# Emptying PSUM bank by bank in three projections, and all weight evacuations of one FFN group on one engine

## What is computed

```python
xn = _layernorm(x, axis=-1)
s = _L0_attn_ref(xn, ...)          # 16 heads, causal softmax, rope on q and k
g = _silu(_L0_ffn_ref(xn, w_gate, w_up, w_down))   # int weights / 127, hidden 3072
x = x + s * g
xn = _layernorm(x, axis=-1)
s = _L1_attn_ref(xn, ...)          # q = x@Wq+bq, k, v alike; softmax(exp(-|q-k|^2)) @ v, then Wo
g = _silu(_L1_ffn_ref(xn, W, b, ids, weights))     # out = sum_k weights[k] * (W[ids[k]] @ x) + bias
x = x + s * g
```

## Time and profile before

| | us |
|---|---|
| median of the 2 runs shown | 3195.87 (3165.48 and 3226.27) |
| profiled execution | 3163.04 |
| its span on the slowest core, core 2 | 3161.5 |
| spans of the 8 cores | 3139.5 to 3161.5 |
| mean granted TensorE clock of the 8 cores | 0.781 to 0.787 |
| TensorE matmuls busy | 2298.7 (73%) |
| VectorE busy | 890.7 (28%) |
| ScalarE busy | 846.7 (27%) |

### The profile page before, as it was taken

How to read it: one execution, slowest core, us unless ns; L and a number is a source line. 1 busy time by engine, 2 the same in 40 slices (tenths; PEclk the granted TensorE clock), 3 DMA queues, 4 the chain that set the end, 5 groups by cost and what they waited for, 6 DMA issues and landing times.

```text
span 3161.5 us, 39763 instructions; the slowest of 8 cores (3139.5 to 3161.5 us)
## 1 busy us (share of the span) xinstructions
PE 2298.7 (73%) x15302; PEld 1261.2 (40%) x15302; DVE 890.7 (28%) x1705; ACT 846.7 (27%) x1181; POOL 78.3 (2%) x148
## 2 busy tenths in 40 slices
PE   2699999984676646787776777347678767887877
PEld 0344444432233213464664666125457322333333
DVE  4344444431232264433223111420110002112122
ACT  2111111112111145464443444201110213222222
POOL 0011111000000000000000000000000000000000
PEclk8799999997878855656556555679889988988899
DMA  4222222202111020101001000441216012011010
GB/s 139 27 34 36 34 33 33 31 1 57 17 17 17 1 53 2 61 2 61 2 1 61 2 2 2 151 109 61 72 57 197 1 27 53 1 54 35 19 54 27
DMA packets 58554, 129.70 MB, mean 41 GB/s; under 512 B 7673, under 2 KB 15867, under 8 KB 55812
## 3 DMA queue, kind: packets, MB, share of 16 engines
q1 hardware_dynamic: 34052, 92.56, 8.7%
q0 software_dynamic: 24320, 34.61, 7.4%
HBM read 142.88 MB, written 18.88 MB: 51 GB/s over the span
## 4 chain that ended last, share of the span: by engine, by line
PE 58%; ACT 16%; DVE 13%; issue 7%; DMA 5%; DVEq 0%; ACTq 0%; SPq 0%; POOL 0%; PEldq 0%; POOLq 0%
PE PS L903 8%; PE PS L737 7%; ACT EB L925 6%; PE PS L1209 6%; PE PS L609 5%; PE PS L618 5%; PE PS L1367 5%; PE PS L1181 4%; PE PS L1436 4%; PE PS L652 4%; PE PS L1292 2%; DVE PS L908 2%; ACT PRJ L745 2%; DVE ACC L663 1%; PE PS L969 1%
## 5 line engine op out<-in xcount | busy, mean ns | idle before, releaser
L903 PE MATMUL PS<-Q,K 64*128 64x128 bf16 x2176 | 274.0, 304 | 126.0 <-ACT EB L925 120.9
L925 ACT ACTIVATE EB<-PS,negBh 128x1152 bf16<-128x1152 f32 (+7 forms) x128 | 204.1, 1594 | 258.0 <-DVE PS L908 242.2
L903 PEld LDWEIGHTS PS<-Q,K 64*128 64x128 bf16 x2176 | 211.4, 135 | 154.8 <-issue 144.1
L1209 PE MATMUL PS<-XN,W1FULL 128*128 128x512 bf16 x768 | 182.3, 399 | 60.6 <-ACT Q L1224 18.7
L652 PE MATMUL PS<-HT,WDT 128*128 128x512 bf16 x768 | 196.4, 392 | 34.8 <-DVE HT L635 21.9
L737 PE MATMUL PS<-XN,WBLK 128*128 128x512 bf16 x768 | 210.4, 442 | 10.1 <-DVE Q L752 5.1
L1181 PE MATMUL PS<-identw,PLAND 128*128 128x128 f32 x1024 | 144.3, 310 | 98.8 <-DMA PLAND<-Wsel 67.3
L908 DVE TENSOR_TENSOR PS<-PS,trinegT 128x128 f32<-128x128 f32 x256 | 76.6, 299 | 440.9 <-PE PS L903 435.0
L1181 PEld LDWEIGHTS PS<-identw,PLAND 128*128 128x128 f32 x1024 | 140.3, 224 | 104.8 <-issue 104.5
L609 PE MATMUL PS<-XN,WGT 128*128 128x512 bf16 x768 | 171.1, 381 | 7.3 <-DVE ACC L663 5.6
L618 PE MATMUL PS<-XN,WUT 128*128 128x512 bf16 x768 | 169.7, 379 | 0.0
(11 more groups left out here) (165 smaller groups left out, 2505.0 us busy)
## 6 DMA issues: line engine op xcount, KB each, us to landing
PLAND<-Wsel SPq DMA_DIRECT2D x64, 512.0 KB, 4.4
XF<-xT SPq DMA_DIRECT2D x8, 1024.0 KB, 12.9
XT<-xT SPq DMA_DIRECT2D x4, 2048.0 KB, 8.7
x1park<-XT SPq DMA_DIRECT2D x32, 256.0 KB
X1CH<-x1park SPq DMA_DIRECT2D x8, 1024.0 KB, 8.5
XT<-x1park SPq DMA_DIRECT2D x4, 2048.0 KB, 8.1
outT<-XT SPq DMA_DIRECT2D x32, 256.0 KB
LAND<-wu POOLq DMA_DIRECT2D x16, 256.0 KB, 3.9
```

Source lines behind the costliest of these rows:

```text
L903: tS = P.op("tensor", lambda t, h=h, gi=gi, tt=tt, off=off: t.matmul(PS[:, off + tt * 128:off + (tt + 1) * 128], head_k(h, ts(tt, 128)), h ...
L925: s.activation(EB2[:, slot, 0:klen], PS[:, 0:klen], AF.Exp, bias=negBh[:, h:h + 1]), inc=True)
L1209: P.op("tensor", lambda t, fc=fc, j=j, n=n: t.matmul(BK(n), W1FULL[:, j, ts(fc, 128)], src_xn[:, j, ts(n, 512)], start=(j == 0), stop=(j = ...
```

## The change

While group 0 is prepared, evac_force makes every evacuation of prep_gen go to ScalarE. In emit_proj_L1 and in the mix projection, the last matmul of each of the four banks raises the semaphore (before: of the fourth bank only); ScalarE waits for each bank by itself; and TensorE waits for bank n's evacuation of the chunk before only at the first matmul (j == 0) into bank n. In the value projection the wait for all four in front of the transposes stays.

```diff
--- before.py
+++ after.py
@@ -478,9 +478,14 @@
     bev67 = {6: None, 7: None}
     p2flip = [0]
 
+    evac_force = [None]
+
     def p2_evac(dst_ap_fn, bk6, ln):
-        eng = "vector" if p2flip[0] == 0 else "scalar"
-        p2flip[0] ^= 1
+        if evac_force[0] is not None:
+            eng = evac_force[0]
+        else:
+            eng = "vector" if p2flip[0] == 0 else "scalar"
+            p2flip[0] ^= 1
         if eng == "vector":
             tok = P.op("vector", lambda v: v.tensor_copy(
                 dst_ap_fn(), BK(bk6, 0, ln)), inc=True)
@@ -550,7 +555,8 @@
                             LANDX(li)[:, ts(j, 128)], ident[:, :],
                             start=True, stop=True), inc=(u == 3))
                     land_guard2[li] = tkT
-                    eng = "vector" if p2flip[0] == 0 else "scalar"
+                    eng = evac_force[0] or (
+                        "vector" if p2flip[0] == 0 else "scalar")
                     P.wait(eng, tkT)
                     tok = p2_evac(
                         lambda dstbuf=dstbuf, hl=idx, b0=b0:
@@ -588,8 +595,10 @@
             yield
 
     ht_cur[0] = tk_var0
+    evac_force[0] = "scalar"
     for _ in prep_gen(0, preland):
         pass
+    evac_force[0] = None
     prev_evac = [None, None]
     for g in range(NG):
         WGTg, WUTg, WDTg = WB[(g + 1) % 2]
@@ -1199,39 +1208,45 @@
     def emit_proj_L1(W_d_, bias_idx, dst_kind, src_xn, bg=None):
         t_w = P.dma("gpsimd", W1FULL[:],
                     W_d_.rearrange("(c p) f -> p c f", p=128), sem="dw")
+        bank_prev = [None] * 4
         for fc in range(EC):
             if bg is not None:
                 next(bg, None)
                 next(bg, None)
             P.wait("tensor", t_w)
+            tkMn = []
             for j in range(EC):
                 for n in range(4):
-                    P.op("tensor", lambda t, fc=fc, j=j, n=n: t.matmul(
+                    if j == 0:
+                        P.wait("tensor", bank_prev[n])
+                    tk = P.op("tensor", lambda t, fc=fc, j=j, n=n: t.matmul(
                         BK(n), W1FULL[:, j, ts(fc, 128)],
                         src_xn[:, j, ts(n, 512)], start=(j == 0),
-                        stop=(j == EC - 1)), inc=(j == EC - 1 and n == 3))
-            tkM = ("tensor", P.sems["tensor"][1])
-            P.wait("scalar", tkM)
+                        stop=(j == EC - 1)), inc=(j == EC - 1))
+                    if j == EC - 1:
+                        tkMn.append(tk)
             bias_ap = bL1[:, bias_idx, fc:fc + 1]
             if dst_kind in ("q1", "k1"):
                 dstb = Q if dst_kind == "q1" else K
                 scl = 2.0 if dst_kind == "q1" else 1.0
                 if dst_kind == "q1":
                     bias_ap = bq2col[:, fc:fc + 1]
-                tkP = None
                 for n in range(4):
-                    tkP = P.op("scalar", lambda s, n=n, fc=fc, dstb=dstb,
-                               bias_ap=bias_ap, scl=scl: s.activation(
-                        dstb[:, fc, ts(n, 512)], BK(n), AF.Identity,
-                        scale=scl, bias=bias_ap), inc=(n == 3))
-                P.wait("tensor", tkP)
+                    P.wait("scalar", tkMn[n])
+                    bank_prev[n] = P.op(
+                        "scalar", lambda s, n=n, fc=fc, dstb=dstb,
+                        bias_ap=bias_ap, scl=scl: s.activation(
+                            dstb[:, fc, ts(n, 512)], BK(n), AF.Identity,
+                            scale=scl, bias=bias_ap), inc=True)
+                tkP = bank_prev[3]
             else:
-                tkP = None
                 for n in range(4):
-                    tkP = P.op("scalar", lambda s, n=n, bias_ap=bias_ap:
-                               s.activation(VFM5[:, ts(n, 512)], BK(n),
-                                            AF.Identity, bias=bias_ap),
-                               inc=(n == 3))
+                    P.wait("scalar", tkMn[n])
+                    bank_prev[n] = P.op(
+                        "scalar", lambda s, n=n, bias_ap=bias_ap:
+                        s.activation(VFM5[:, ts(n, 512)], BK(n),
+                                     AF.Identity, bias=bias_ap), inc=True)
+                tkP = bank_prev[3]
                 P.wait("tensor", tkP)
                 for bi, b0 in enumerate(range(0, TTILES, 4)):
                     bk = 4 + (bi % 2)
@@ -1286,21 +1301,24 @@
     P.wait("tensor", t_bm)
     P.barrier()
 
+    bank_prev2 = [None] * 4
     for fc in range(EC):
+        tkMn = []
         for j in range(EC):
             for n in range(4):
-                P.op("tensor", lambda t, fc=fc, j=j, n=n: t.matmul(
+                if j == 0:
+                    P.wait("tensor", bank_prev2[n])
+                tk = P.op("tensor", lambda t, fc=fc, j=j, n=n: t.matmul(
                     BK(n), WMIXT[:, j, ts(fc, 128)], XN1[:, j, ts(n, 512)],
-                    start=(j == 0), stop=(j == EC - 1)),
-                    inc=(j == EC - 1 and n == 3))
-        tkM = ("tensor", P.sems["tensor"][1])
-        P.wait("scalar", tkM)
-        tkP = None
+                    start=(j == 0), stop=(j == EC - 1)), inc=(j == EC - 1))
+                if j == EC - 1:
+                    tkMn.append(tk)
         for n in range(4):
-            tkP = P.op("scalar", lambda s, n=n, fc=fc: s.activation(
+            P.wait("scalar", tkMn[n])
+            bank_prev2[n] = P.op("scalar", lambda s, n=n, fc=fc: s.activation(
                 G[:, fc, ts(n, 512)], BK(n), AF.Silu,
-                bias=bmixcol[:, fc:fc + 1]), inc=(n == 3))
-        P.wait("tensor", tkP)
+                bias=bmixcol[:, fc:fc + 1]), inc=True)
+    P.wait("tensor", bank_prev2[3])
     P.barrier()
     tbq2 = P.op("vector", lambda v: v.tensor_add(
         bq2col[:, :], bL1[:, 0, :], bL1[:, 0, :]), inc=True)
```

## The result

The changed kernel takes 3081.8 us (median), against 3166.7 before. The ratio is 0.9723, 95% interval 0.9700 to 0.9747: 80 to 95 us won. (Runs in which one die was disturbed are left out of it.) The profiled execution took 3083.3 us, span 3081.1 on core 3. The forecast was 3084, that is 79 us off the profiled execution of the kernel before; from that to the profiled execution after it are 79.8 us. (Four projections were changed, key, value, mix and query, where the title says three.)

A forecast was written before the change was run, and what follows sets the result against it. TensorE carries 58% of the critical chain, the rest mostly its waits for one other engine. Gains of 16.1, 21.2, 5.2 and 19.5 us (62.0) plus 17 of clock, 79 off 3163.0, gave 3084 us, range 3072 to 3096.

The forecast's parts named there:

- Part 1: First layernorm: group 0's evacuations all on ScalarE, so gate matmuls start when VectorE ends; 16.1 us won.
- bound of 80: First layernorm: group 0's weights ready by about 80 us, with 13 us to spare before VectorE ends.
- rival of the held loads: First layernorm: POOL's loads held until VectorE ends at 93.27 us; 2.3 us won instead of 16.1, 3098 us; chance 0.10.
- Part 2: Key projection: ScalarE's evacuations hide behind the premix, seven gaps vanish; 21.2 us, plus 6.2 of clock.
- Part 3: Value projection: only ScalarE's earlier start, 0.65 us eight times, is won; 5.2 us, plus 4 of clock.
- clock term: Layer 1's four projections: shorter or vanished gaps give back time of slow matmul stretches; 17 us, bounds 0 and 28.8.
- Parts 4 and 5: Mix and query projections: earlier ScalarE start and bank-by-bank TensorE restart; 9.75 us each, plus 3.5 and 3.3 of clock.
- The structure: Mix and query, without clock: 1.30 of each 2.66 us gap won, blocks every 8.4 us instead of 9.7; 19.5 us together.
- The rival that the clock gives nothing back: Layer 1's projections: gaps go but slow stretches stay; 3101 us, or 3113 with new slow blocks; chance 0.12.
- The rival of the slow restart: Mix and query: single matmuls at restart leave the clock at 1.2 GHz, costing 85 us; 3186 us; chance 0.05.

The follow-up runs named there:

- 27.3 alone: Kernel before with only the key projection's signals and waits per bank; 27.3 us won in its stage, ratio 0.9943 (0.9907 to 0.9978).
- 10.1 alone: Kernel before with only the value projection's signals and waits per bank; 10.1 us won in its stage, ratio 0.9983 (0.9959 to 1.0006).
- the late restart: Changed kernel, but in mix and query TensorE waits for all four banks before the next block; 3101.3 and 3103.5 us.
- the late ScalarE: Changed kernel, but in mix and query ScalarE starts only when all four banks are complete; 3097.2 and 3102.5 us.

## Why the prediction was right, point by point

- **Part 1** (16.1 us): 17.4 won up to the first gate matmul, 0.9 given back after it; the first gate block took 9.80 us behind a long idle stretch, against 8.54, 1.26 more where I took 1.1. ScalarE was done at 74 us, earlier than the bound of 80. The rival of the held loads fell: between 58 and 76 us, under VectorE's two-input operations, the nine loads of group 0 issued from POOL landed in medians of 3.2 to 4.3 us (changed kernel, DMA issues: KB each, median us to landing), as against 3.9 in the earlier trace rows. The four loads of group 1, issued within 2 us of each other from 73.3 us on, took longer, 4.8 to 7.9, but landed under the layernorm as well. Of the rule of the Trainium skill weighed there ("SBUF — State Buffer", section "SBUF: two separate sides"), the half about two-input operations is the one that this trace agrees with.

```profile
LANDB<-wd POOLq DMA_DIRECT2D x4, 96.0 KB, 3.3
LAND<-wd POOLq DMA_DIRECT2D x4, 96.0 KB, 3.2
LAND<-wu POOLq DMA_DIRECT2D x1, 256.0 KB, 4.3
...
LANDB<-wu POOLq DMA_DIRECT2D x1, 256.0 KB, 7.9
```

- **Part 2** (21.2 + 6.2): 27.2 in the stage, 27.3 alone. Both terms held: the 208 premix matmuls are busy 24.4 us, where 24.9 was full speed and 31.1 was measured before.
- **Part 3** (5.2 + 4): 7.3 in the whole change, 10.1 alone. The pause is 2.13 us, as said. The clock term was too large: counted as in the earlier trace rows, 209 premix matmuls take 35.5 us, where 37.7 stood before and 25.1 is full speed. So 2.2 us came back, where I took 4.
- **Parts 4 and 5** (19.5 + 6.8): 31.1. The structure is exact, 8.44 us from block to block against 9.73. The clock term was too small: I let some slow blocks stay because the pauses only became shorter, and none of 112 stayed. Beyond the structure's 19.5 us the two stages won 11.6, where I took 6.8; about 1 us of that is the query's first block, the one behind the barrier: 9.8 us before, 8.8 after (medians of the six cores). The reason I gave, single matmuls between, is the one that the late restart and the late ScalarE bear out. ScalarE's train stays unbroken: four evacuations take 2.42 us with the waits between them too, and the new waits on TensorE cost nothing that shows.
- **The rival that the clock gives nothing back** (3101 to 3113 us) has fallen: no block of 112 is slow, the key premix is at full speed, and the stages of key, mix and query won 17.6 us beyond what the shorter gaps explain.
- **The rival of the slow restart** (3186 us) has fallen: TensorE got one matmul per 0.6 us for 2.4 us, and the clock stayed at 1.00. What the Trainium skill ("TensorE: Matmul & The Clock Gate", section "A second HAM failure mode: psum-queue depth-cycling") reports as oscillation with cycling banks did not occur in this pattern, where the clock stayed at 1.00. It did with the unbroken pauses of 2.01 and 2.66 us (0.91 and 0.92), and less with 0.93 us and single matmuls (0.97), all over the same four banks.
- **What was luck.** The parts' stages sum to 82 us, 3 more than forecast: mix and query gave 4.8 too much, value 1.9 too little. The last stage took 6 back in the profiled pair by its own scatter, which no term of mine foresaw. That the profiled pair differs by 79.8 us, against 79, is partly owed to that. The timed medians say 3166.7 - 3081.8 = 85 us, the ratio 88.

## What to carry to other kernels

When one engine fills four banks and another empties them, signal and wait for each bank, and let the loop order complete one bank after the other: in mix and query signals per bank took the block-to-block time from 9.73 to 8.44 us, the loop order took it on to 6.91, at no cost in matmul time. Look next at every wait for "all four"; here the same kind of edit, with a split multiplication and one copy less, won 158 us in three projections that this change left alone, nearly twice the whole change. And an operation queued behind a long, unrelated train on its engine is worth moving to an idle engine even if it is tiny: one evacuation of 0.7 us held TensorE for 39 us.

## What the runs showed of the hardware that was not expected

- An unbroken pause of 2.01 us left 70 of 112 following blocks slow, one of 2.66 us 47. The same waiting as the 2.01 us, broken up by three single matmuls, left 18 (0.93 us ahead of the first); with 0.28 us ahead of the first there was none.
- In the value projection, on the six cores, 30 of 36 premixes were slow behind an unbroken pause of 2.0 to 2.4 us (changed kernel; 5.0 to 6.2 us for 32 matmuls) and 6 of 36 behind one of about 1.04 (n as the outer loop; the others 3.79).
- Which blocks are slow repeats from core to core: before, the second, third and sixth of the mix on all eight. What decides it, the runs do not tell.
- Most slow blocks lose 1.4 to 1.7 us where the stage is running: 8.54 against 7.07 behind a pause of 2.66 us, 8.75 behind one of 2.01. The worst lost nearly 3.
- Eight matmuls in a row into one bank run at the same 0.216 us each as alternating over four banks.
